# A four-layer graph network on one core: the order of PE, ACT and POOL work in the first layer and at the three borders

## What is computed

```python
x = _layernorm(x + _L0_gnn_ref(x, edge_index, edge_weight, edge_attr_64, ...))   # attention
x = _layernorm(x + _L1_gnn_ref(x, src, dst, ...))                                 # mean, two linear maps, relu
x = _layernorm(x + _L2_gnn_ref(x, src, dst, edge_type_8, ...))                    # one matrix for each of 8 relations
x = _layernorm(x + _L3_gnn_ref(x, src, dst, edge_type_3, node_type_3, ...))       # messages by edge type, update by node type
```

## Time and profile before

| what | us |
|---|---|
| median of 3 runs (1653.00 to 1656.04) | 1655.96 |
| the profiled execution's own time | 1652.15 |
| its span | 1650.4 |
| busy: PE / DVE / ACT / POOL | 1388.8 / 1419.0 / 1110.9 / 1230.3 |
| mean granted clock of PE | 0.93 |

### The profile page before, as it was taken

The page is one execution under the profiler, slowest core; times in us unless marked ns, Lnnn a source line. Parts: engine busy times, 40 slices in busy tenths (PEclk is TensorE's granted clock), DMA queues, the critical chain, the costliest instruction groups (busy, mean ns, idle before and its releaser), DMA issues.

```text
span 1650.4 us, 22899 instructions
## 1 busy us (share of the span) xinstructions
PE 1388.8 (84%) x6078; PEld 890.6 (54%) x6078; DVE 1419.0 (86%) x3056; ACT 1110.9 (67%) x2769; POOL 1230.3 (75%) x910
## 2 busy tenths in 40 slices
PE   3788877788778868777776899999996899999995
PEld 2455554555545546666665555555553455555552
DVE  5899899999899879999998799999995677777773
ACT  1678788887788787888888577777774344444441
POOL 7888888877777857888874567777778488888873
PEclk9798888988889879999998999999998899999997
DMA  7344444434444256767675455556554344344320
GB/s 172 94 100 102 111 109 110 112 91 115 111 113 105 58 139 177 189 179 192 182 187 149 131 149 164 156 157 165 151 133 111 83 97 96 96 97 97 96 70 20
DMA packets 165797, 205.06 MB, mean 124 GB/s; under 512 B 66825, under 2 KB 97920, under 8 KB 165668
## 3 DMA queue, kind: packets, MB, share of 16 engines
q1 hardware_dynamic: 108068, 179.45, 40.0%
q0 software_dynamic: 57600, 24.15, 9.0%
HBM read 147.12 MB, written 70.80 MB: 132 GB/s over the span
## 4 chain that ended last, share of the span: by engine, by line
PE 44%; DVE 32%; ACT 12%; issue 10%; POOL 1%; DMA 1%; SPq 0%; DVEq 0%; POOLq 0%; ACTq 0%
PE po L1391 23%; DVE bst L756 8%; DVE masked L969 6%; PE pt L1380 5%; PE pc L1500 3%; PE po L1386 3%; ACT x L1074 3%; DVE run L831 2%; PE po L1451 2%; DVE y L796 2%; DVE po L799 2%; DVE sel L802 2%; DVE po L800 2%; ACT do L1074 2%; PE pa L1672 1%
## 5 line engine op out<-in xcount | busy, mean ns | idle before, releaser
L536 POOL DMA_INDIRECT xs<-target_rows,slot_all x236 | 322.2, 1365 | 140.9 <-issue 60.9
L1074 ACT ACTIVATE x<-y,nmr,rst 125x128 f32<-125x128 f32 x800 | 322.5, 483 | 29.6 <-issue 18.4
L1391 PE MATMUL po<-wnt,rt 128*125 128x384 f32 x800 | 297.4, 518 | 0.0
L1380 PE MATMUL pt<-ident,x 125*128 125x125 f32 x800 | 122.3, 276 | 110.5 <-issue 110.5
L1391 PEld LDWEIGHTS po<-wnt,rt 128*125 128x125 f32 x800 | 162.7, 206 | 96.9 <-issue 21.2
L1391 PE MATMUL po<-wnt,run 128*125 128x384 f32 x600 | 201.5, 486 | 0.0
L543 POOL DMA_INDIRECT out_rows<-do,last_all x100 | 146.5, 1465 | 63.0 <-issue 40.6
L1380 PEld LDWEIGHTS pt<-ident,x 125*128 125x128 f32 x800 | 93.1, 145 | 148.4 <-issue 147.1
L536 POOL DMA_INDIRECT xs<-in_x,src_all x100 | 143.2, 1432 | 34.7 <-issue 33.8
L1074 ACT ACTIVATE do<-yd,nmr,rst 125x128 f32<-125x128 f32 x400 | 163.5, 483 | 5.4 <-DVE nmr L781 4.6
L1074 ACT ACTIVATE res<-sel,nmr,rst 125x128 f32<-125x128 f32 x400 | 163.7, 484 | 2.6 <-DVE nmr L781 1.8
(11 more groups left out here) (190 smaller groups left out, 3035.1 us busy)
## 6 DMA issues: line engine op xcount, KB each, us to landing
xin<-in_x SPq DMA_DIRECT2D x100, 224.0 KB
out_rows<-res SPq DMA_DIRECT2D x100, 224.0 KB
source_rows<-so SPq DMA_DIRECT2D x75, 224.0 KB
target_rows<-do SPq DMA_DIRECT2D x75, 224.0 KB
xs<-source_rows SPq DMA_DIRECT2D x59, 224.0 KB
same<-same_d SPq DMA_DIRECT2D x50, 250.0 KB
rel<-in_etype SPq DMA_DIRECT2D x50, 250.0 KB
xd<-target_rows SPq DMA_DIRECT2D x46, 224.0 KB
```

Of the source, the lines that this page charges most:

```text
L536: return nc.gpsimd.indirect_dma_start(out=to, out_offset=None, in_=table, in_offset=bass.IndirectOffsetOnAxis(ap=index, axis=0), bounds_ch ...
L1074: last = A(to[:, j, :], y[:, j, :], ACT.Identity, scale=rst[s][:, k:k + 1], bias=nmr[s][:, k:k + 1])
L1380: last = nc.tensor.transpose(tile_of(to, j), rows_[:, j, :], ident[0:R, 0:R])
L1391: last = mm(po[0:R, j * 512:j * 512 + NT * D], left(j), wnt[:, k, :, :].rearrange("k t d -> k (t d)"), start=start, stop=stop, skip_group_ ...
```

## The change

Phase 1 on POOL: from c = 20 on, where no slots are left, each turn also issues three gathers of types, 15 in all, so that only two are left behind phase 2. Phase 0 on ACT: the copy of targets moves from the end of a turn to the next one, behind its roots. Phase 0 on PE: biases and types' products of chunk 2c+1 move ahead of the turn of targets, its z products ahead of the score product. Border 1/2 on ACT: in the last turn the copies rt and xt of block 48 move ahead of and behind the source rows, and the roots of block 50 ahead of the two results; `chain_rows` is `dense_chain` without its roots. Border 2/3 on PE: `turns2(0)` moves ahead of the dense products of block 75. Border 3/4 on ACT: the copy of the second sources moves ahead of `dense_chain(105)`.

```diff
--- before.py
+++ after.py
@@ -633,6 +633,9 @@
                     if i % T == 0:
                         pool.wait_ge(s_slot[k], 16 * T * (n - 1))
                     slots1(i, i + 1, s_slot[k])
+                if SOONER * T + 3 * c >= EC * T:
+                    types2(typed, typed + 3)
+                    typed += 3
             types2(typed, typed + 2 * T)
             typed += 2 * T
 
@@ -1123,8 +1126,12 @@
 
             def dense_chain(d):
 
+                first_roots(chain_of(d) % 2, 4)
+                chain_rows(d)
+
+            def chain_rows(d):
+
                 k = chain_of(d)
-                first_roots(k % 2, 4)
                 act.wait_ge(s_ln, k + 1)
                 rows_of(d, k % 2, (2, 0))
                 results_of(d, k % 2, 1)
@@ -1190,6 +1197,8 @@
             for c in range(EC):
                 s = chain_of(2 * c) % 2
                 first_roots(s, 8)
+                if c >= 1 and there(c + 1):
+                    evacuate_targets(c + 1, 0, 0, dt, ACT.Copy)
                 if there(c + 1):
                     slopes0(c + 1)
                 act.wait_ge(s_ln, c + 1)
@@ -1217,12 +1226,13 @@
                     target_rows0(c - 1, s, 7)
                     act.wait_ge(s_tail, 1)
                     target_rows0(c, TAIL, 0)
+                    evacuate_rt(2 * EC - 2)
                     source_rows0(c, s)
+                    evacuate_xt(2 * EC - 2)
+                    first_roots(chain_of(2 * EC) % 2, 4)
                     results_of(2 * c, s, 2)
                     results_of(2 * c + 1, s, 3)
-                if there(c + 2):
-                    evacuate_targets(c + 2, 0, 0, dt, ACT.Copy)
-            only_dense(2 * EC)
+            chain_rows(2 * EC)
             evacuate_dense(2 * EC - 1)
             evacuate_sources(0, 1, 7, 1.0)
             evacuate_targets(0, 1, 7, dt, ACT.Copy, 1.0)
@@ -1350,8 +1360,8 @@
             evacuate_sources(0, 3, 0)
             messages3(0)
             targets3(0)
+            evacuate_sources(1, 3, 0)
             dense_chain(NC + 2 * LAG - 1)
-            evacuate_sources(1, 3, 0)
             act.wait_ge(s_x1, NC)
             act.wait_ge(s_ln, chain_of(NC - 1) + 1)
             type_rows3(0)
@@ -1553,10 +1563,16 @@
                     if there(c + 2):
                         score_sources(c + 2)
                     turn_xt(2 * c + 1)
+                    if 2 * c + 1 >= LAG:
+                        type_products(2 * c + 1)
+                    else:
+                        pe.wait_ge(s_read, 2 * c + 4)
+                        biased_slots()
                     if there(c + 2):
                         turn_targets0(c + 2)
+                    z_products(2 * c + 1).then_inc(s_z, 1)
+                    if there(c + 2):
                         score_targets(c + 2)
-                    dense_products(2 * c + 1)
 
             def turn_sources1(c):
                 q = ph[1]
@@ -1628,9 +1644,9 @@
 
             d = block_of(1, EC)
             dense_turns(d - 2)
-            dense_products(d - 2)
             pe.wait_ge(ph[1]["rd"], EC)
             turns2(0)
+            dense_products(d - 2)
             relations2(0, range(REL // 2))
             turn_rt(d - 1)
             relations2(0, range(REL // 2, REL))
```

## The result

The changed kernel takes 1657.92 us (median of 16 runs, 1656.24 to 1661.50) against 1653.78 for the kernel before in the same session: a ratio of 1.0027, 95% interval 1.0020 to 1.0035. The forecast of 1634 had the wrong sign, and the range (1611 to 1650) missed.

What follows compares the result with a forecast made beforehand. The first layer was taken as bound by DVE's turns of 23.0 us, the last by PE. Savings of 5 + 1.8 + 3.3 + 10.1 = 20.2 off 1652.15 give 1632, plus 2 makes 1634; own range 1625 to 1641, wider range 1611 to 1650.

Steps and rivals of the forecast that it cites:

- Border 1/2: Between layers 1 and 2: rt and xt copied around the source rows save ACT's two waits, 1.8 us less.
- Border 2/3: Between layers 2 and 3: turning the first sources ahead of the dense products, against later gathers, gives 3.3 us less.
- Border 3/4: Ahead of the last layer: POOL's earlier start 3.3 and the earlier copy of second sources 6.8, together 10.1 us less.
- the term of the clock in the first layer: First layer: PE's clock falls in two of three turns at 1.2 us each, making a turn 22.8.
- The loop at full clock: First layer: with PE's clock at its upper level, the loop of ACT and PE sets a turn at 22.0 us.
- rival (c): First layer: back products stand alone, the clock falls every turn, 24.3 a turn, 1666 us in all; chance 0.08.
- ACT's roots first: First layer, ACT: roots ahead of the copy of targets remove the wait before L778, 0.9 us a turn.
- Rival (b): First layer gives nothing, the wait moves from L778 to L842; only part of the borders counts, 1643 us; chance 0.2.
- POOL as a floor at 21.8: First layer: POOL's 13 gathers and scatters take 21.8 us a turn, capping this part's gain near 25 us.
- The late gathers: Border 2/3: 15 gathers of types run before, so the third layer's first gathers start at 903.4 instead of 900.88.
- the 7.64: Border 2/3: time from the first gathers' start to the turn of sources, putting that turn at 911.0.
- rival (d): First sources wait for late gathers with dense products behind; other waits change names, first layer as before: 1654 us; chance 0.07.

Runs made afterwards that it cites:

- the filled kernel: The changed kernel with the four transposes of the back products repeated three more times (12 more, outputs unchanged): 1646.30 us, ratio 0.9968.
- the fastest kernel: First layer's order of the kernel before, rt copied early, borders as changed, 20 unread transposes ahead of the turn of targets: 1605.81 us, ratio 0.9715.

## Why the prediction was wrong

**The step that failed** is the term of the clock in the first layer: "I take one in two of three turns at 1.2: 22.8". Both its factors were too small. The fall came in every turn, at the same place, and it cost 2.0 us (23.89 less the 21.88 of the filled kernel's turns without one) instead of 1.2, so a turn took 23.85. The price weighs more: a fall in every turn at 1.2 would have given 23.2. The prediction gives no working for its 1.1 to 1.5. In the filled kernel's turn without a fall, ACT's waits for the turned x and sources are nearly gone:

```profile
369.29 0.59 ACT L1120 ACTIVATE xt<-pt 128x500 f32<-128x500 f32 x1 [0.20 <-PE pt L1390]
...
370.79 0.57 ACT L1147 ACTIVATE st<-pt 128x500 f32<-128x500 f32 x1
```

Against the 1.53 and 0.55 of the changed kernel that is 1.88 of the 2.0: both waits lie behind half-speed work and follow one another. The loop at full clock was right: put at 22.0, and the turns without a fall took 21.88, with 1.3 us of repeated transposes in them. The mechanism was described as rival (c) and put at 0.08. How often it falls was taken as a chance in each turn. A repeated turn is no draw: it brings the same thin stretch each time, and here the turn settled on a length at which the fall returns to the same place; other kernels of the study settled on a pattern of two, four or more turns.

21 turns × 0.85 = 17.9, and 4.1 more in the first ones, which the prediction left out, make the 21.9 lost where 5 were to be won. The 4.1 is the fourth copy of scores, 83.43 against 79.37; in the traces with the loop as before it falls between 79.37 and 81.62, so some 2 us of it are no more than the spread between traces. A slip beside it: 21 × 0.2 is 4.2, not 5, and 21 × 1.0 is 21, not 22; and the earlier trace rows show one thin stretch with the clock at 0.50 behind it, where the prediction speaks of two.

The Trainium skill's remedy for such bursts (TensorE: Matmul & The Clock Gate, HAM oscillation), named in the prediction against this change, held. Real work put beside the back products was worth 27 us in the new order, and filling the thin stretch 44 (1654.8 to 1610.3); in the old order filling was worth 28 (1633.6 to 1605.8).

**ACT's roots first** (0.9 a turn to be won, queued work "costs nothing"): the wait named did go, 18.1 to 0, but with PE's old order 22.2 came in its place (12.1 ahead of L844, 10.1 more ahead of y). What was late next was the scores' copy, behind a copy of targets that now came later. Rival (b) had it, at 0.2.

**POOL as a floor at 21.8**: too high. In the fastest kernel it issued 273 in 445.3 us, 13 in 21.2: 362.4 busy and 273 × 0.30 between them, so without a pause, but quicker (1.63 us each) than in the stretch that I read (1.68).

**Border 1/2** (1.8 less): 2.4 at the first sums, 0.3 by the sixth; alone it costs 1.7. The step took PE's earlier start as free and did not ask what the clock does once PE has run dry behind it.

**Border 2/3** (3.3 less): 1.8. The late gathers were sized well: 924.22 less the 21.55 of shift is 902.7, 1.8 late, where 2.5 was forecast. The term that failed is the 7.64 from the first gather to the turned sources, borrowed from the last layer. POOL's and PE's timelines of after:

```profile
924.22 1.27 POOL L536 DMA_INDIRECT xs<-target_rows,slot_all  x1 [0.30 <-issue]
```

```profile
931.96 0.94 PE L1390 MATMUL pt<-ident,x 125*128 125x125 f32 x4 [4.24 <-issue]
935.84 1.06 PE L1390 MATMUL pc<-ident,xs 125*128 125x125 f32 x4 [2.94 <-issue]
```

It took 11.6, PE waited 2.94 for the sources, and the dense products stood behind them: rival (d)'s picture for this border. With nothing in the way (first gather at 902.23, turn at 913.70) it took 11.5 too.

**Border 3/4** (10.1 less): 14.7. Both terms were too small: POOL 3.3 (6.6 alone in the trace), since the stored targets landed 2 us sooner than I took and a fall of the clock went with PE's wait; the copy 6.8 (7.4 to the first updated rows). The same two timelines of after at this border:

```profile
1276.66 1.27 POOL L536 DMA_INDIRECT xdb<-target_rows,slot_all  x1 [18.82 <-DMA target_rows<-do]
```

```profile
1285.22 0.62 PE L1390 MATMUL pt<-ident,xdb 125*128 125x125 f32 x4 [0.75 <-issue]
1286.58 1.10 PE L1688 MATMUL pa<-st,wet 128*128 128x500 f32 x2 [0.74 <-ACT st L1147]
...
1291.99 1.11 PE L1688 MATMUL pa<-st,wet 128*128 128x500 f32 x2 [0.68 <-ACT st L1147]
```

The waits of 4.09 and 7.40 are 0.75 and 0.68, and POOL idles 18.82 where it had no pause. The borders together gave 16.7 by the milestones against 15.2 forecast. That the two are close is partly luck: 4.6 too little at one border against 3.0 too much at the other two. Only the first layer turned the sign.

**Left open.** The parts alone add up to 17.9 us (6.4 + 8.9 + 4.3 - 1.7) and all together measure 15.1; with intervals of some 2 us each that may be nothing. Why the gathers at border 2/3 need 11.5 us and those of the last layer 7.6 was not tried. The trace of after has a gather's median time from issue to landing at border 2/3, 5.7 us; in 924.20 to 935.80 the DMA engines were 0.78 busy and moved 211 GB/s, where in the stretch of before that the 7.64 comes from they were 0.29 busy and moved 84. Contention is likely, but not shown. Whether DVE or POOL holds the 21.2 us was not told apart: neither then has a wait of any size.

## What to carry to other kernels

In a loop whose engines meet at waits, look at the granted clock stretch by stretch before an edit takes small work away from big work on PE. Falls come back in a fixed pattern, here in every turn, in every second or in all but one of five or six, so price one for each repetition until a trace shows otherwise. When such a loop won't get shorter although a wait was removed, fill PE's thin stretch as a test; if more work makes it faster, the clock was what held it. And price what follows the wait that is removed: a wait on the ring of engines changes its name as long as the ring is as long as before.

## What the hardware showed that was not expected

- The length of a turn settles where the falls repeat. The changed kernel and the one with ACT's old order differ in their waits but both end at 23.89 a turn; the kernel before goes through 22.41, 23.15, 23.18 and 23.42 again and again, and so does the kernel with rt copied early (22.42, 23.16, 23.20, 23.41), with 1.64 us less ahead of PE's turn of x.
- Taking a wait out of such a loop can do next to nothing: 1657.9 to 1654.8 with rt early in the new order. Adding 12 transposes then takes off 44 us.
- A thin stretch can be filled in part: with rt early and in the new order, 4 more transposes leave a fall in every second turn and 12 in none of the 20 turns traced.
